# Degrees of a graph aggregation from sums over source tiles made on GpSimd, and one fp32 product with ones for each block

## The chip, the cores and the metric

The kernel runs on one core of a Trainium2 chip. The metric is the device time of one execution in microseconds (us). The core has five engines that work at the same time and are kept in step by semaphores: TensorE (PE), VectorE (DVE), ScalarE (ACT), GpSimd (POOL) and SyncE (SP, which only issues transfers).

## The reference

Two graph layers follow each other on 1250 nodes with 512 features and 20000 edges. The part that the change touches is the first layer's mean over incoming edges: the sum of the messages of a destination is divided by its degree, the number of edges that end in it, but at least 1.

```
msg = xn[edge_index[0]]                                          # xn: batch-normed relu(layernorm(x))
agg = segment_sum(msg, edge_index[1], num_segments=N)
deg = segment_sum(ones((E,)), edge_index[1], num_segments=N)
agg = agg / maximum(deg, 1.0)[:, None]
conv_out = relu(agg @ W_conv + b_conv)
...                                                              # linear attention over the first 256 nodes, h_attn
x = x + batchnorm(conv_out + h_attn + h)                         # first layer
h = maximum(layernorm(x), 0.0)
agg = segment_sum(h[src], dst, num_segments=N)                   # second layer
x = x + relu(batchnorm(relu(batchnorm(((1 + eps) * h + agg) @ W1 + b1)) @ W2 + b2))
```

## The kernel before

**The adjacency.** The 1250 nodes are ten tiles of 125 (`T`, `L`). The kernel builds the matrix `AT`, of 125 partitions by ten source tiles by 1250 destinations: how many edges go from a source to a destination, in fp16. Aggregation then is a product with `AT`. The destinations are cut into 25 windows of 50 (`NW`, `W`), and each window `t` goes through three engines. DVE writes 0/1 rows: `S` for the source's lane (L976) and eight rows of `ring` for tile and destination (L980, called one-hots here). PE multiplies them into counts (eight products, `ring,S`). ACT copies the counts into `AT` (L584), which raises the semaphore `s_at` by one. `ATlo` holds what fp16 can't; its products run only where some count is that large (`If_lt(big_r, most_r)`), which these edges don't ask for.

**The slots.** Between the counts of two windows PE does other work. The table `SLOTS` (L76) names it, slot `t` before the counts of window `t`. The names that matter here: `G7`, `G8`, `G9` are the convolution products of node tiles 7 to 9 (12 products each); `R6` and so on take the rounding remainder of such a tile; `UQ`, `QT`, `MX`, `KV`, `O`, `TA`, `WO` are steps of the attention; `A00` is the aggregate of feature block 0 over destination block 0 (20 products), `D0`, `D1`, `D2` are the degrees of the three destination blocks (`COLS`: 0 to 449, 450 to 849, 850 to 1249), `F1` and `F2` the mean square of the second layer's two weights. D0 stands in slot 18, D1 in slot 23, D2 in the list `LAST` behind the windows.

**What feeds G.** For tile `i`, ACT norms the tile (`hn`, L681), DVE splits it in `hn_hi` and `hn_lo` (L1094, L1095, in the function `normed_parts`), and PE's `G` waits for the second (`s_hns`). DVE's list in window `t` is: `S` and the eight one-hots of window `t + 1`, the split of tile `t - 7`, then the slot's reductions. In window 14 these are the maxima of `UQ2` (`qmax`, `nbq`), which ACT's exponentials (`qf`) wait for; ACT norms tile 8 behind them.

**A degree.** PE multiplies a matrix of ones with `AT` for each of the ten source tiles and sums in PSUM, so that all 128 partitions hold the degree (L1552). ACT copies it to `rdb` (D0, D1), DVE takes the maximum with 1 and the reciprocal (L1034, L1035). Every engine works through its own list in the order in which the program writes it, and waits on semaphores.

**GpSimd** does the scales of norms: for the first layer, then for the two weights (`mean_w`, `scale_w`, L517, L518, behind `F1` and `F2`), then small things of the later stages, with two large ones: the rows `x1 + h` (L529) and the low halves `a_lo` (L557).

Of the kernel before, what the change touches and what calls it, by code (L numbers as in the profile page):

```python
# [5 lines left out]
F32 = mybir.dt.float32  # L6
# [5 lines left out]
ALU = mybir.AluOpType  # L12
# [3 lines left out]
P = 128  # L16
# [3 lines left out]
N, D, HID, E = 1250, 512, 1024, 20000  # L20
# [5 lines left out]
T = 10  # L26
L = N // T
# [6 lines left out]
W = 50  # L34
# [118 lines left out]


SQ1_AT, HIGH1_AT = (20, 21), (23, 24)
RAW = [name for slot in SLOTS for name in slot if name[0] == "A"]
OUT_TILES = [(0, 4), (4, 8), (8, 10)]

# [33 lines left out]
def gnn_kernel(nc, x, src, dst, params, eps, w_conv, wq, wk, wv, wo, proj, w1, w2, out):  # L192
    with ExitStack() as ctx:
        sems = {}

        def sem(name):
            if name not in sems:
                sems[name] = ctx.enter_context(nc.semaphore(name))
            return sems[name]

        def place(name, shape, dt, kib):

            pad = nc.sbuf_tensor(name + "_at", [P, int(kib * KIB)], U8)
            pad.__enter__()
            it = nc.sbuf_tensor(name, shape, dt)
            t = it.__enter__()
            it.__exit__(None, None, None)
            pad.__exit__(None, None, None)
            return t
# [4 lines left out]
        ones16 = place("ones16", [P, P], F16, 3.25)  # L214
        zeros16 = place("zeros16", [P, 1], F16, 3.5)
# [6 lines left out]
        ones32 = place("ones32", [P, 1], F32, 7.9375)  # L222
# [41 lines left out]
        AT = place("AT", [L, T, N], F16, 8)  # L264
        ATlo_all = place("ATlo", [L, T * N], F8, 32.5)
        ATlo = ATlo_all[:].rearrange("p (t n) -> p t n", t=T)
# [44 lines left out]
        st_1 = place("st_1", [P, FB, T, 6], F32, 108)  # L311
        tmpr = place("tmpr", [P, 2, COLS[0][1]], F32, 109.1875)
        aggf = place("aggf", [P, 4, COLS[0][1]], F32, 130.75)
        rdb = place("rdb", [P, N], F32, 146)
        x1 = place("x1", [L, T, D], F32, 154)

        w1_s = [place(f"w1_s{half}", [P, 2, HID], F32, at) for half, at in enumerate((92, 162))]
# [26 lines left out]
        def open_group(eng, name):  # L344
            bank, turn = PLACE[name]
            if turn:
                eng.wait_ge(free[bank], turn)
            return banks[bank]
# [97 lines left out]
        def _(pool):  # L446
            own = Own(pool, sem("own_pool"))
# [63 lines left out]
            factor = wscale[:, 0:1].broadcast_to([P, FB])  # L511
            pool.tensor_tensor(bn_0[:, 0, :], bn_s[:, 0:FB], factor, ALU.mult).then_inc(sem("s_bn0"), 1)
            pool.tensor_tensor(bn_0[:, 1, :], bn_t[:, 0:FB], factor, ALU.mult).then_inc(sem("s_bn0"), 1)
            for layer in range(2):
                pool.wait_ge(sem(f"s_mean_w{layer}"), 1)
                m, s = mean_w[layer], scale_w[layer]
                own.step(pool.tensor_scalar(m[:, 1:2], m[:, 0:1], 1e-30, None, ALU.add))  # L517
                pool.tensor_tensor(s[:, 0:1], m[:, 1:2], minus_half[:, 0:1], ALU.pow).then_inc(sem(f"s_scale_w{layer}"), 1)  # L518
            for f in range(FB - 1):
                pool.wait_ge(sem("s_mv2"), f + 1)  # L520
                batch_scales(f, 1, pcol("n2g", f), pcol("n2b", f), sem("s_bn2"))
# [18 lines left out]
            n = 0  # L540
# [848 lines left out]
        def _(pe):  # L1389
            def mm(o, l, r, start, stop):  # L1390
                return pe.matmul(o, l, r, start=start, stop=stop, skip_group_check=True)  # L1391
# [11 lines left out]
            ps = open_group(pe, "codes")  # L1403
            for a, k in enumerate((1, 2)):
                pe.transpose(ps[0:CH, a * NCH:a * NCH + P], code_r[:, k, 0, :], ident[:])
                ins = pe.transpose(ps[0:CH, a * NCH + P:(a + 1) * NCH], code_r[0:rest, k, 1, :],
                                   ident[0:rest, 0:rest])
            close_group(ins, "codes")
            ps = open_group(pe, "ranges")
            for a in range(2):  # L1410
                mm(ps[0:NH, a * NCH:a * NCH + P], wm[:, a, 0:1].broadcast_to([P, NH]), ident[:], True, True)
                ins = mm(ps[0:NH, a * NCH + P:(a + 1) * NCH], wm[0:rest, a, 1:2].broadcast_to([rest, NH]),
                         ident[0:rest, 0:rest], True, True)
# [42 lines left out]
            def attention(name):  # L1456
# [4 lines left out]
                if name in ("F1", "F2"):  # L1461
                    layer = int(name[1]) - 1
                    pe.wait_ge(sem(f"s_ssq_w{layer}"), 2)
                    ps = open_group(pe, name)[:, 0:1]
                    for half in range(2):
                        ins = mm(ps, ssq_w[layer][:, half:half + 1].broadcast_to([P, P]), ones32[:], half == 0, half == 1)
                    close_group(ins, name)
                    return
                if name[0] == "G":
# [9 lines left out]
                    ps = open_group(pe, name)  # L1479
                    n = 0  # L1480
                    if i == 0:
                        for k in range(FB):
                            ins = mm(ps[0:L, :], hn[:, 0, k, :], wC[:, k, :], k == 0, k == FB - 1)
# [59 lines left out]
                elif name[0] == "D":  # L1543
# [4 lines left out]
                    if name == "D0":  # L1548
                        released("P")
                        pe.load([most_r], most[0:1, 0:1])  # L1550
                    ps = open_group(pe, name)
                    ins = accumulate([(ps[:, 0:w], [(ones16[0:L, :], AT[:, k, c0:c0 + w]) for k in range(T)],  # L1552
                                       [(ones16[0:L, :], ATlo[:, k, c0:c0 + w]) for k in range(T)])])[0]
                elif name[0] == "N":
                    a = int(name[1])
                    for half in range(2):
# [83 lines left out]
            def accumulate(groups):  # L1640

                for ps, pairs, _ in groups:
                    mm(ps, *pairs[0], True, False)
                with pe.If_lt(big_r, most_r):
                    for ps, _, extra in groups:
                        for l, r in extra:
                            mm(ps, l, r, False, False)
                pe.end_ifs()
                last = []
                for ps, pairs, _ in groups:  # L1650
                    for n, (l, r) in enumerate(pairs[1:]):
                        ins = mm(ps, l, r, False, n == len(pairs) - 2)
                    last.append(ins)
                return last
# [187 lines left out]
```

## Time and profile before

| | us |
|---|---|
| median of 3 runs | 367.86 (367.85 to 368.13) |
| the profiled execution | 367.88, of which span 366.0 |
| PE busy | 352.8 (96%) |
| DVE busy | 239.9 (66%) |
| ACT busy | 185.7 (51%) |
| GpSimd busy | 94.6 (26%) |
| mean granted TensorE clock | 0.999 of full speed |

The span goes from the first to the last instruction. Shares are of the span. A product's row lasts longer than the distance to the next one, since products are pipelined: what one costs is read from start to start. A line such as L1391 is that of a helper through which nearly all products go, so rows are told apart by their operands.

### The profile page before, as it was taken

The numbers are of one execution on the slowest core, as the hardware profiler recorded it, in microseconds if no ns is written. First come the engines' busy times: TensorE is split into PE (matmuls) and PEld (weight loads), VectorE is DVE, ScalarE is ACT, GpSimd is POOL, SyncE is SP. The second block draws the span as 40 slices with busy tenths as digits, with TensorE's granted clock in tenths as the row PEclk, the third lists the DMA queues.
The fourth block names the chain that finished last, engine by engine and source line by source line (L and its number), as shares of the span: only waits on it lengthen the run. The fifth ranks groups of instructions, "written<-read, shape, count | busy, mean of one in ns | idle before, by whom it ended". The sixth has DMA issues, their size and how long they took to land.

```text
span 366.0 us, 6163 instructions
## 1 busy us (share of the span) xinstructions
PE 352.8 (96%) x2062; PEld 225.3 (62%) x2062; DVE 239.9 (66%) x650; ACT 185.7 (51%) x311; POOL 94.6 (26%) x163
## 2 busy tenths in 40 slices
PE   7999999989999999999998999999999999999994
PEld 3786655767767666768555665455555555565562
DVE  5889999997877886857987886522465353422324
ACT  1447647779587157465436677411443644333132
POOL 8132120000000000100042678722277565101100
PEclk9999999999999999999999999999999999999999
DMA  6990303300000000024900000000000000010223
GB/s 180 281 298 21 118 2 122 113 3 1 3 4 3 3 3 3 2 71 167 257 19 1 2 0 3 4 2 0 0 3 0 2 0 0 2 49 23 70 56 84
DMA packets 13538, 18.03 MB, mean 49 GB/s; under 512 B 1839, under 2 KB 6895, under 8 KB 13491
## 3 DMA queue, kind: packets, MB, share of 16 engines
q1 hardware_dynamic: 12538, 17.21, 16.4%
q8 instruction: 25, 0.41, 0.5%
q10 hardware_dynamic: 953, 0.23, 0.3%
q14 instruction: 22, 0.18, 0.2%
HBM read 14.88 MB, written 2.56 MB: 48 GB/s over the span
## 4 chain that ended last, share of the span: by engine, by line
PE 72%; DVE 14%; ACT 6%; issue 4%; DVEq 2%; POOL 1%; DMA 0%; SPq 0%; ACTq 0%; POOLq 0%
PE bank L1391 68%; DVE ring L980 2%; DVE st_row L930 1%; ACT hn L681 1%; PE bank L1421 1%; PE bank L1781 1%; PE bank L1743 1%; PE bank L1607 1%; DVE kmax L996 1%; DVEq L1129 1%; DVE st L1087 1%; DVE wC_lo L1241 1%; POOL ln_s L483 1%; DVE hn_lo L1095 1%; DVE hl L1271 1%
## 5 line engine op out<-in xcount | busy, mean ns | idle before, releaser
L1391 PE MATMUL bank<-AT,hh 125*128 125x400 f16 (+1 forms) x240 | 81.0, 340 | 1.5 <-DVE hl L1271 1.2
L1391 PE MATMUL bank<-AT,hl 125*128 125x400 f16 (+1 forms) x240 | 80.8, 339 | 0.0
L980 DVE TENSOR_SCALAR ring<-iota_code,code 125x250 f16<-125x250 f16 x200 | 46.1, 306 | 1.8 <-issue 1.8
L1391 PEld LDWEIGHTS bank<-AT,hh 125*128 125x128 f16 x240 | 23.2, 97 | 20.2 <-DVE hl L1271 1.6
L1391 PEld LDWEIGHTS bank<-AT,hl 125*128 125x128 f16 x240 | 23.4, 97 | 18.0 <-issue 0.2
L1391 PE MATMUL bank<-ring,S 125*128 125x250 f16 x200 | 33.5, 310 | 0.0
L1391 PE MATMUL bank<-a_hi,w_hi 128*128 128x400 f16 (+1 forms) x96 | 32.6, 340 | 0.0
L1391 PE MATMUL bank<-agg_hi,w_hi 128*128 128x400 f16 (+1 forms) x96 | 32.6, 340 | 0.0
L1391 PE MATMUL bank<-a_hi,w_lo 128*128 128x400 f16 (+1 forms) x96 | 32.5, 339 | 0.0
L1391 PE MATMUL bank<-agg_hi,w_lo 128*128 128x400 f16 (+1 forms) x96 | 32.5, 339 | 0.0
L1391 PE MATMUL bank<-agg_lo,w_hi 128*128 128x400 f16 (+1 forms) x96 | 32.5, 339 | 0.0
L1391 PE MATMUL bank<-a_lo,w_hi 128*128 128x400 f16 (+1 forms) x96 | 32.5, 339 | 0.0
L517 POOL TENSOR_SCALAR mean_w<-mean_w 128x1 f32<-128x1 f32 x2 | 0.9, 448 | 121.3 <-ACT mean_w L584 121.3
L1391 PEld LDWEIGHTS bank<-ring,S 125*128 125x128 f16 x200 | 25.8, 145 | 9.0 <-issue 1.7
L853 ACT ACTIVATE zr<-bank,par,undo_w 128x400 f32<-128x400 f32 (+1 forms) x24 | 16.0, 690 | 23.5 <-POOL a_lo L557 17.1
L557 POOL TENSOR_TENSOR a_lo<-zr,a_hi 128x1250 f16<-128x1250 f32 x7 | 22.0, 3142 | 16.7 <-DVE a_hi L1313 16.7
L1082 DVE BATCH_NORM_STATS2 st_f<-zr 128x6 f32<-128x400 f32 (+1 forms) x24 | 13.5, 588 | 18.1 <-ACT zr L853 18.1
L877 ACT ACTIVATE ur<-bank,par,undo_w 128x400 f32<-128x400 f32 (+1 forms) x12 | 8.2, 697 | 32.7 <-PE bank L1391 22.2
L492 POOL TENSOR_TENSOR bn_tmp<-var_eps,minus_half 128x1 f32<-128x1 f32 (+1 forms) x15 | 8.7, 581 | 54.1 <-DVE var_eps L1101 54.1
L976 DVE TENSOR_TENSOR S<-iota_lane,slo 125x1024 f16<-125x1024 f16 x25 | 18.6, 744 | 5.9 <-PE bank L1391 3.5
L483 POOL TENSOR_TENSOR ln_s<-ln_tmp,minus_half 125x1 f32<-125x1 f32 x20 | 14.5, 724 | 24.3 <-DVE ln_tmp L926 24.3
L584 ACT ACTIVATE AT<-bank 125x500 f16<-125x500 f32 x25 | 15.2, 606 | 10.6 <-PE bank L1391 10.4
(230 smaller groups left out, 708.5 us busy)
## 6 DMA issues: line engine op xcount, KB each, us to landing
w_s<-w SPq DMA_DIRECT2D x4, 1024.0 KB, 5.1
x_in<-x SPq DMA_DIRECT2D x5, 448.0 KB
x<-x SPq DMA_DIRECT2D x2, 1120.0 KB
out<-x SPq DMA_DIRECT2D x6, 224.0 KB
wB<-wk SPq DMA_DIRECT2D x1, 1024.0 KB, 8.7
wA<-wq SPq DMA_DIRECT2D x1, 1024.0 KB, 13.9
wC<-w_conv SPq DMA_DIRECT2D x1, 1024.0 KB, 16.3
wB<-wv SPq DMA_DIRECT2D x1, 1024.0 KB, 7.6
```

What stands on the lines that cost most here:

```text
L483: own.step(pool.tensor_tensor(s, ln_tmp[:, 0, i:i + n], minus_half[0:L, 0:n], ALU.pow))
L492: own.step(pool.tensor_tensor(bn_tmp[:, 1, k:k + n], var_eps[:, k:k + n], minus_half[:, 0:n], ALU.pow))
L557: pool.tensor_tensor(a_lo[:, b, :], zr[:, b % 2, :], a_hi[:, b, :], ALU.subtract)\
L584: return act.activation(o, i, ACT.Copy, scale=scale)
L681: ins = act.activation(hn[:, i % 2, f, :], hT[:, f, i * L:(i + 1) * L], ACT.Identity, bias=b[:, f:f + 1], scale=s[:, f:f + 1])
L853: ins = act.activation(zr[:, b % 2, c0:c0 + w], ps[:, 0:w], ACT.Identity, bias=pcol("b1", b), scale=undo_w[0][:, 0:1])
L877: ins = act.activation(ur[:, f % 2, c0:c0 + w], ps[:, 0:w], ACT.Identity, bias=pcol("b2", f), scale=undo_w[1][:, 0:1])
L930: own.step(dve.bn_stats(st_row[:, i % 2, :], x_tile(i)))
L976: dve.tensor_tensor(S[:, slot], iota_lane[0:CH], a, ALU.is_equal)
L980: return dve.tensor_scalar(ring[:, slot, j, a:b], iota_code[0:CH, a:b], code[:, bass.ds(c + j, 1)], float(-CODES * t), ALU.subtract, ALU.i ...
L1082: return dve.bn_stats(st_f[:, f, ci, :], ap)
L1391: return pe.matmul(o, l, r, start=start, stop=stop, skip_group_check=True)
```

## The change

GpSimd now sums `AT` over the ten source tiles, for 100 destinations at a time (13 groups, the last of 50), in fp32. It takes four sums: five tiles plus five tiles (`deg_1`), two plus two of these (`deg_2`), the two results, and the fifth. The result is `degs`, one value for each of 125 lanes and 1250 destinations, in the memory of `rdb`. A group begins when the windows that it reads are copied, and not before 14 are (`DEGREES_FROM`). `s_degs` counts the groups. PE waits for the groups of its block and makes one fp32 product of `degs` with ones in place of ten fp16 products; a product with one column of zeros closes the group in PSUM, since the `ATlo` products between the two are left out or not by a branch. On GpSimd the scale of the first of the second layer's weights now stands behind the eleventh group, that of the other behind the last.

```diff
--- before.py
+++ after.py
@@ -153,6 +153,8 @@
 
 
 SQ1_AT, HIGH1_AT = (20, 21), (23, 24)
+
+DEGREES_FROM = 14
 RAW = [name for slot in SLOTS for name in slot if name[0] == "A"]
 OUT_TILES = [(0, 4), (4, 8), (8, 10)]
 
@@ -311,7 +313,11 @@
         st_1 = place("st_1", [P, FB, T, 6], F32, 108)
         tmpr = place("tmpr", [P, 2, COLS[0][1]], F32, 109.1875)
         aggf = place("aggf", [P, 4, COLS[0][1]], F32, 130.75)
+
         rdb = place("rdb", [P, N], F32, 146)
+        degs = place("degs", [L, N], F32, 146)
+        deg_1 = place("deg_1", [L, T // 2, 2 * W], F32, 150.90625)
+        deg_2 = place("deg_2", [L, 2, 2 * W], F32, 152.875)
         x1 = place("x1", [L, T, D], F32, 154)
 
         w1_s = [place(f"w1_s{half}", [P, 2, HID], F32, at) for half, at in enumerate((92, 162))]
@@ -511,11 +517,30 @@
             factor = wscale[:, 0:1].broadcast_to([P, FB])
             pool.tensor_tensor(bn_0[:, 0, :], bn_s[:, 0:FB], factor, ALU.mult).then_inc(sem("s_bn0"), 1)
             pool.tensor_tensor(bn_0[:, 1, :], bn_t[:, 0:FB], factor, ALU.mult).then_inc(sem("s_bn0"), 1)
-            for layer in range(2):
+            def weight_scale(layer):
                 pool.wait_ge(sem(f"s_mean_w{layer}"), 1)
                 m, s = mean_w[layer], scale_w[layer]
                 own.step(pool.tensor_scalar(m[:, 1:2], m[:, 0:1], 1e-30, None, ALU.add))
                 pool.tensor_tensor(s[:, 0:1], m[:, 1:2], minus_half[:, 0:1], ALU.pow).then_inc(sem(f"s_scale_w{layer}"), 1)
+
+            def source_sums(n, c0, w):
+
+                half = T // 2
+                if n:
+                    pool.wait_ge(sem("s_degs"), n)
+                pool.wait_ge(sem("s_at"), max(DEGREES_FROM, -(-(c0 + w) // W)))
+                own.step(pool.tensor_tensor(deg_1[:, :, 0:w], AT[:, 0:half, c0:c0 + w], AT[:, half:T, c0:c0 + w], ALU.add))
+                own.step(pool.tensor_tensor(deg_2[:, :, 0:w], deg_1[:, 0:2, 0:w], deg_1[:, 2:4, 0:w], ALU.add))
+                own.step(pool.tensor_tensor(deg_2[:, 0, 0:w], deg_2[:, 0, 0:w], deg_2[:, 1, 0:w], ALU.add))
+                pool.tensor_tensor(degs[:, c0:c0 + w], deg_2[:, 0, 0:w], deg_1[:, 4, 0:w], ALU.add)\
+                    .then_inc(sem("s_degs"), 1)
+
+            groups = [(c0, min(2 * W, N - c0)) for c0 in range(0, N, 2 * W)]
+            for n, (c0, w) in enumerate(groups):
+                source_sums(n, c0, w)
+                if c0 + w == 1100:
+                    weight_scale(0)
+            weight_scale(1)
             for f in range(FB - 1):
                 pool.wait_ge(sem("s_mv2"), f + 1)
                 batch_scales(f, 1, pcol("n2g", f), pcol("n2b", f), sem("s_bn2"))
@@ -1548,9 +1573,14 @@
                     if name == "D0":
                         released("P")
                         pe.load([most_r], most[0:1, 0:1])
-                    ps = open_group(pe, name)
-                    ins = accumulate([(ps[:, 0:w], [(ones16[0:L, :], AT[:, k, c0:c0 + w]) for k in range(T)],
-                                       [(ones16[0:L, :], ATlo[:, k, c0:c0 + w]) for k in range(T)])])[0]
+                    pe.wait_ge(sem("s_degs"), -(-(c0 + w) // (2 * W)))
+                    ps = open_group(pe, name)[:, 0:w]
+                    mm(ps, ones32[0:L, 0:1].broadcast_to([L, P]), degs[:, c0:c0 + w], True, False)
+                    with pe.If_lt(big_r, most_r):
+                        for k in range(T):
+                            mm(ps, ones16[0:L, :], ATlo[:, k, c0:c0 + w], False, False)
+                    pe.end_ifs()
+                    ins = mm(ps[:, 0:1], ones16[0:L, :], zeros16[0:L, 0:1], False, True)
                 elif name[0] == "N":
                     a = int(name[1])
                     for half in range(2):
```

PE's list where D0 stands (`degs` against `ones`), before:

```order
L1391 MATMUL bank<-hh,neg_id 125x512 [waits s_gh]
L1550 TENSOR_LOAD most [waits s_lo1,free6,s_lo0,s_at]
L1391 MATMUL bank<-AT,ones 128x450 [waits free7]
L1644 COMPARE_AND_BRANCH
L1391 MATMUL bank<-ATlo,ones 128x450 x10
L1644 UNCONDITIONAL_BRANCH
L1391 MATMUL bank<-AT,ones 128x450 x9
L1678 TENSOR_LOAD win [waits s_lo1,s_at]
```

and now:

```order
L1416 MATMUL bank<-hh,neg_id 125x512 [waits s_gh]
L1575 TENSOR_LOAD most [waits s_lo1,free6,s_lo0,s_at]
L1416 MATMUL bank<-degs,ones 128x450 [waits free7,s_degs]
L1579 COMPARE_AND_BRANCH
L1416 MATMUL bank<-ATlo,ones 128x450 x10
L1579 UNCONDITIONAL_BRANCH
L1416 MATMUL bank<-zeros,ones 128x1
L1708 TENSOR_LOAD win [waits s_lo1,s_at]
```

Nine products in a row are gone behind the branch, a closing one of one column stands there, and the first waits for GpSimd too.

GpSimd's list between the first layer's scales (`bn`) and those of the weights, before:

```order
L512 TENSOR_TENSOR bn<-bn_s,wscale 128x4 [waits s_bn1]
L513 TENSOR_TENSOR bn<-bn_t,wscale 128x4
L517 TENSOR_SCALAR mean_w<-mean_w 128x1 [waits s_mean_w0]
L518 TENSOR_TENSOR scale_w<-mean_w,minus_half 128x1 [waits own_pool]
L517 TENSOR_SCALAR mean_w<-mean_w 128x1 [waits s_mean_w1]
```

and now (the first two groups of sums, and the end of the eleventh):

```order
L519 TENSOR_TENSOR bn<-bn_t,wscale 128x4
L532 TENSOR_TENSOR deg<-AT 125x500 [waits s_at]
L533 TENSOR_TENSOR deg<-deg 125x200 [waits own_pool]
L534 TENSOR_TENSOR deg<-deg 125x100 [waits own_pool]
L535 TENSOR_TENSOR degs<-deg 125x100 [waits own_pool]
L532 TENSOR_TENSOR deg<-AT 125x500 [waits s_at,s_degs]
...
L535 TENSOR_TENSOR degs<-deg 125x100 [waits own_pool]
L523 TENSOR_SCALAR mean_w<-mean_w 128x1 [waits s_mean_w0]
L524 TENSOR_TENSOR scale_w<-mean_w,minus_half 128x1 [waits own_pool]
L532 TENSOR_TENSOR deg<-AT 125x500 [waits s_at,s_degs]
```

Eleven groups of four sums stand ahead of the first weight's scale, two more ahead of the second's. The lists of DVE and ACT stay as they were.

## Rows read from the trace of the kernel before

**Rows 1.** Page: chain by engine; then busy time (instructions) of two stretches.
```profile
PE 72%; DVE 14%; ACT 6%; issue 4%; DVEq 2%; POOL 1%; DMA 0%; SPq 0%; ACTq 0%; POOLq 0%
...
core 0: us, PE busy (x) PEld busy (x) DVE busy (x) ACT busy (x) POOL busy (x), PEclk, DMA share, GB/s
95.70:119.20 23.50, 22.70 (x140) 16.69 (x139) 18.33 (x62) 16.86 (x38) 0.00 (x0) 1.00 0.01 3
119.20:191.30 72.10, 72.10 (x444) 48.31 (x443) 57.30 (x124) 34.47 (x48) 5.88 (x14) 1.00 0.23 67
```

**Rows 2.** Timeline of PE at D0, D1, D2: start us, us, operation, idle before.
```profile
119.29 2.06 PE L1391 MATMUL bank<-AT,ones 125*128 125x450 f16 x10
121.19 1.33 PE L1391 MATMUL bank<-ring,S 125*128 125x250 f16 x8
...
148.59 1.86 PE L1391 MATMUL bank<-AT,ones 125*128 125x400 f16 x10
150.28 0.33 PE L1391 MATMUL bank<-AT,hh 125*128 125x400 f16 x1
...
176.05 1.85 PE L1391 MATMUL bank<-AT,ones 125*128 125x400 f16 x10
```

**Rows 3.** Timeline of PE: the fp32 products of WO0, WO1.
```profile
165.39 7.07 PE L1391 MATMUL bank<-attnT,wA 128*128 128x256 f32 x32
...
172.29 0.34 PE L1391 MATMUL bank<-AT,hh 125*128 125x400 f16 x1
```

**Rows 4.** Timeline of GpSimd: a sum with one element, one with 1250.
```profile
261.61 0.19 POOL L494 TENSOR_TENSOR bn_tmp<-mv_f,bn_s 128x1 f32<-128x1 f32 x1
261.88 0.19 POOL L495 TENSOR_TENSOR bn_t<-par,bn_tmp 128x1 f32<-128x1 f32 x1
...
281.07 2.56 POOL L557 TENSOR_TENSOR a_lo<-zr,a_hi 128x1250 f16<-128x1250 f32 x1 [2.39 <-DVE a_hi L1313]
```

**Rows 5.** Timelines of DVE and GpSimd where they work at the same time.
```profile
223.72 0.69 DVE L1271 TENSOR_TENSOR hl<-hring,hh 125x512 f16<-125x512 f32 x1
226.74 1.33 DVE L1271 TENSOR_TENSOR hl<-hring,hh 125x512 f16<-125x512 f32 x1 [2.33 <-ACT hh L826]
...
225.04 2.49 POOL L529 TENSOR_TENSOR x<-x,hring 125x512 f32<-125x512 f32 x2
...
52.45 0.36 POOL L495 TENSOR_TENSOR bn_t<-par,bn_tmp 128x4 f32<-128x4 f32 x1
```

**Rows 6.** Timeline of DVE, windows 14 to 17.
```profile
98.48 0.68 DVE L1095 TENSOR_TENSOR hn_lo<-hn,hn_hi 128x500 f16<-128x500 f32 x1
...
101.39 0.16 DVE L1012 SCALAR_TENSOR_TENSOR nbq<-diag,qmax 128x2 f32<-128x2 f32 x1
102.17 0.69 DVE L976 TENSOR_TENSOR S<-iota_lane,slo 125x1024 f16<-125x1024 f16 x1 [0.62 <-PE bank L1391]
...
106.26 0.42 DVE L1094 CAST hn_hi<-hn 128x500 f16<-128x500 f32 x1 [1.53 <-ACT hn L681]
106.72 0.68 DVE L1095 TENSOR_TENSOR hn_lo<-hn,hn_hi 128x500 f16<-128x500 f32 x1
...
110.12 0.68 DVE L1095 TENSOR_TENSOR hn_lo<-hn,hn_hi 128x500 f16<-128x500 f32 x1
...
112.62 1.85 DVE L980 TENSOR_SCALAR ring<-iota_code,code 125x250 f16<-125x250 f16 x8 [0.20 <-issue]
```

**Rows 7.** Timelines of PE (first products of G7, G8, G9) and ACT.
```profile
102.07 0.38 PE L1391 MATMUL bank<-wC_hi,hn_hi 128*125 128x512 f16 x1
...
107.51 0.39 PE L1391 MATMUL bank<-wC_hi,hn_hi 128*125 128x512 f16 x1
...
112.37 0.38 PE L1391 MATMUL bank<-wC_hi,hn_hi 128*125 128x512 f16 x1
...
95.13 0.60 ACT L584 ACTIVATE AT<-bank 125x500 f16<-125x500 f32 x1 [0.57 <-PE bank L1391]
...
102.55 0.47 ACT L646 ACTIVATE qf<-bank,nbq 128x256 f32<-128x256 f32 x1
```

**Rows 8.** Timeline of DVE at the first layer's end.
```profile
191.55 0.58 DVE L1179 TENSOR_TENSOR tmpr<-bank,rdb 128x400 f32<-128x400 f32 x1 [0.96 <-PE bank L1391]
```

## The prediction, made before the changed kernel ran

> **What bounds the kernel now.** I read the chain of waits first: 72% of the span runs through PE, most of it through its products [rows 1]. Then the table of busy time by stretch. From 119.20 to 191.30 us PE is busy 72.10 of 72.10 us, so time taken off its list there comes off the run, and any wait put before it is added to the run. From 95.70 to 119.20 us PE is busy 22.70 of 23.50 us and DVE 18.33, while GpSimd does nothing at all. Both lie at the full granted clock (1.00). The reader should see two things in these rows: PE is the bound through the whole change, and DVE, in the stretch where GpSimd is to start working, has only 5.2 us in which it is idle.
>
> **What leaves PE.** The three degree groups D0, D1 and D2 are ten fp16 products each [rows 2]: 119.29 to 121.19 is 1.90 us, 148.59 to 150.28 is 1.69, and D2 at 176.05 has the row of D1's shape, so 1.69 too. Together 5.28 us. The branch inside them costs nothing visible: 1.90 us for 4500 columns is 0.42 ns a column, as in the products around it.
>
> **What PE gets.** One fp32 product for each group. Its price is read from the last attention products: 32 records of 256 columns, two to a product, from 165.39 to 172.29, so 6.90 / 16 = 0.431 us for 256 columns or 1.68 ns a column [rows 3]. 1250 columns cost 2.10 us. The closing product has one column and a weight load of its own. From above it is bounded by one of the eight products of 250 columns (1.33 / 8 = 0.17 us [rows 2]), from below by nothing. I take 0.10, as what loading the weights leaves of it: 0.3 us for three. Total 2.4, **saving 2.9 us** (between 2.7 and 3.2). The branch now stands behind the fp32 product; it costs nothing as long as that product (0.76 us, four times the one that covered it) hides it, and at most a few tenths if not.
>
> **What GpSimd gets.** Four sums for each of 13 groups. One element takes 0.19 us, 1250 take 2.56 [rows 4], so 1.90 ns an element over 0.19: 1.14 us for 5x100 elements, 0.57 for 2x100, 0.38 and 0.38 for the two of 100. With 0.08 between (the small rows stand 0.27 apart, at 261.61 and 261.88, less 0.19) a group is 2.8 us. The inputs of the first sum are fp16, which no GpSimd row has; its price lies between 0.6 (half) and 1.3. GpSimd is busy 0.00 and 5.88 us of the two stretches [rows 1], so the time is there. Groups 0 to 6 all become due at once, when the copy of window 13 (from 95.13 us) is in [rows 7], and the rest follow two windows apart.
>
> **Do the new waits of PE end late?** D0 wants group 4. Alone, five groups take 14 us from 95.7 and end at 110, 9 us before D0. D1 wants group 8, due before D0 and used 29 us later. D2 wants group 12, due with the last copy of counts, before the output products of the attention, which alone take 6.9 us. The scale of the second layer's first weight now stands behind group 10 on GpSimd; that group is due a window before the mean for which the scale waits. I put all four at zero; if a group were late, the counts of the next window, and with them everything on PE, would queue behind D0.
>
> **What it does to DVE.** This is the term that decides. GpSimd's adds and DVE meet once in this trace [rows 5]. DVE's difference of two SBUF tensors takes 0.69 us alone and took 1.33 when it began at 226.74 inside an add of GpSimd that ended at 225.04 + 2.49 = 227.53. It lost 0.64 and so came free about 0.14 before the add's end. So DVE stood still while GpSimd read. Does that hold for DVE's one-hots (`ring`), the bulk of its work? A product of four elements on GpSimd took 0.36 instead of some 0.2 when only one-hots ran beside it [rows 5], so a one-hot does hold GpSimd up; that GpSimd holds a one-hot up is not in the trace, since nothing long ran on GpSimd then. I take it that it goes both ways.
>
> The Trainium skill, "SBUF — State Buffer", section "Who interferes with whom", speaks against this change: DVE and GpSimd share one pair of ports under an exclusive lock, DVE instructions with two SBUF inputs and one-source ones in a two-port mode (tensor_scalar among them) contend, and the one that came second waits for the whole instruction. The trace agrees for two inputs (0.64 us lost); no row shows the one-hot as the second. By the rule my forecast stands; if it ended at two-input instructions, the second case below would.
>
> Now the walk. A group of sums blocks DVE for 1.00 + 0.43 + 0.24 + 0.24 = 1.9 us (each sum less 0.14), and in each gap of 0.22 us DVE gets one or two one-hots through (0.23 each: 1.85 / 8) [rows 6].
> - Window 14. When GpSimd begins, eight one-hots and the two halves of the split of tile 7 (hn_hi, hn_lo) stand before DVE. About six sums slip between them: 3.3 us, of which 0.4 falls on idle time. The split ends at 102.0 instead of 98.48 + 0.68 = 99.16 [rows 6]. PE wants it at 102.07 (G7) [rows 7]: covered. But the maxima of UQ2 end at 104.4 instead of 101.55; ScalarE takes them from 102.55, and its norm of tile 8 moves by about 2.
> - Window 15. DVE begins at 104.5 instead of 102.17 and loses another 2.3 us in the one-hots, less the 1.53 us for which it waited before tile 8 [rows 6]. The split of tile 8 is 3.1 us late. G8 followed it by 0.11 us (107.40 to 107.51) [rows 6, 7]: **PE loses 3.1**.
> - Window 16. Ten more contending instructions, 3.4 us more: the split of tile 9 is 6.6 late. It ended at 110.80, 1.57 us before G9 at 112.37. **PE has lost 5.0.**
> - Later. The seven due groups run out near 121 us. The one-hots of window 18 ended at 114.47 and PE counts them at 121.19, 6.7 us later, which covers DVE's further delay, and the six late groups meet a DVE that waits for PE. At the end of the stretch DVE waited 0.96 us for the last A product [rows 8]; DVE's list there moves with D0 and D1, so D2's saving of 1.0 uses that up and costs nothing above 0.1.
>
> Sum: 5.0 - 2.9 = **2.1 us slower**. The profiled run took 367.88 us (span 366.0) and the median of the runs is 367.86, so the forecast is 367.88 + 2.1 = 370.0, and the same for the median. The term of 5.0 is soft: with sums of 0.9/0.45/0.3/0.3 us the same walk gives 2.5, with 1.25 us for the first sum 5.8. The case's own range is 367.9 to 372.
>
> **Rivals.**
> - Faster: GpSimd doesn't hold one-hots up, only the two-input instructions. Then in each window at most two of them wait, mostly under idle time, and PE loses some 0.3: 367.88 - 2.9 + 0.3 = 365.3. For it: no row shows a one-hot held. Against it: the four elements that a one-hot did hold up.
> - Faster or equal, held but mildly: the fp16 sums are cheap, near 0.6 to 0.9 us, or more one-hots slip into a gap. PE loses 1 to 2.5: 366.0 to 367.5.
> - Slower still: if the gap between two sums is a little shorter than a one-hot, exactly one gets in. The split of tile 7 is then 5.2 us late and PE stalls there already, 2.3; by G9 it has lost 10, net 375. It decides from a gap under 0.2 us, and I have 0.22. Stalls of 3 us may also lower TensorE's clock, which costs further time; the stretch of the walk holds 0.8 us of idle PE in all, at full clock [rows 1], so no row prices that.
> - The change doing nothing: excluded, since PE's list is shorter by 24 products.
>
> **Chances.** The forecast 0.42, faster without the hold 0.33, mild hold 0.15, strict alternation 0.10. Two in ten may lie outside: the range is 364.8 to 373.5. A measurement can tell about 0.2% (0.74 us) from no change. Faster than 367.1: all of the second case and half of the mild one, 0.40. Within 0.2%: the other part of the mild one and the foot of the forecast, 0.12. Slower: 0.48.
>
> **What would show it.** In the new profile: D0 to D2 at 0.8 to 0.9 us each (right or wrong for the 2.9). The first sum at 1.1 us on GpSimd. In 96 to 118 us the `ring` rows of DVE at two or three times 1.85 us for eight, and PE idle before G8 and G9, put down to DVE's hn_lo. If the `ring` rows stay at 1.85, the walk is wrong and the time is near 365.3. If GpSimd's sums take two or three times their price while DVE keeps its pace, DVE wins the port each time: also 365.3, unless group 4 then misses D0.

## The result, and the profile after

The changed kernel takes **372.61 us** (median of 4 runs, 372.60 to 373.80) where the kernel before takes 368.0 (4 runs, 367.85 to 368.35): a ratio of 1.0125, 95% interval 1.0093 to 1.0156. It is slower, as forecast, and 2.6 us above the 370.0 that the prediction named, inside its range of 364.8 to 373.5, though not inside the 367.9 to 372 that it gave its main case. The profiled execution took 372.6 us with a span of 370.8, against 367.88 and 366.0: 4.8 us more.

The busy time of the stretches of [rows 1] in the changed kernel, with two stretches more (columns as there):

```profile
core 0: us, PE busy (x) PEld busy (x) DVE busy (x) ACT busy (x) POOL busy (x), PEclk, DMA share, GB/s
95.70:119.20 23.50, 20.34 (x106) 13.67 (x106) 22.92 (x51) 13.96 (x33) 21.22 (x29) 0.93 0.01 2
119.20:191.30 72.10, 72.10 (x448) 49.38 (x447) 64.31 (x133) 36.08 (x54) 23.20 (x33) 1.00 0.23 67
112.00:114.00 2.00, 2.00 (x6) 1.12 (x5) 2.00 (x6) 0.00 (x0) 1.88 (x2) 0.50 0.00 0
235.00:240.00 5.00, 5.00 (x22) 2.36 (x21) 1.30 (x3) 1.65 (x3) 3.51 (x4) 0.78 0.00 0
```

In the first stretch DVE is now busy 22.92 of 23.50 us, for fewer instructions (51 for 62), GpSimd 21.22, and PE gets through 106 products where it did 140. The last two rows are new: TensorE's granted clock falls to half, once at 112 us and once near 235.

DVE's timeline, which answers to [rows 6]:

```profile
96.24 2.98 DVE L1005 TENSOR_SCALAR ring<-iota_code,code 125x250 f16<-125x250 f16 x8 [0.19 <-issue]
99.13 1.24 DVE L1119 CAST hn_hi<-hn 128x500 f16<-128x500 f32 x1
100.41 0.98 DVE L1120 TENSOR_TENSOR hn_lo<-hn,hn_hi 128x500 f16<-128x500 f32 x1
...
104.86 3.26 DVE L1005 TENSOR_SCALAR ring<-iota_code,code 125x250 f16<-125x250 f16 x8
108.04 0.61 DVE L1119 CAST hn_hi<-hn 128x500 f16<-128x500 f32 x1
108.69 1.39 DVE L1120 TENSOR_TENSOR hn_lo<-hn,hn_hi 128x500 f16<-128x500 f32 x1
```

Eight one-hots take 2.98 to 3.26 us where they took 1.85, and the splits 1.24 + 0.98 and 0.61 + 1.39 where they took 0.42 + 0.68. Durations (ns) of all 200 one-hots, least, median and most; then three single one-hots out of the row of 104.86, and the two sums that they met:

```profile
L1005 DVE TENSOR_SCALAR ring<-iota_code,code x200: 274/290/1064, 15.4 to 154.5; 125x250 f16<-125x250 f16 x100
...
105.46 1.06 DVE L1005 TENSOR_SCALAR ring<-iota_code,code 125x250 f16<-125x250 f16 x1
106.45 0.34 DVE L1005 TENSOR_SCALAR ring<-iota_code,code 125x500 f16<-125x500 f16 x1
106.71 0.63 DVE L1005 TENSOR_SCALAR ring<-iota_code,code 125x250 f16<-125x250 f16 x1
...
105.28 1.16 POOL L532 TENSOR_TENSOR deg<-AT 125x500 f32<-125x500 f16 x1
106.52 0.73 POOL L533 TENSOR_TENSOR deg<-deg 125x200 f32<-125x200 f32 x1
```

The one-hot that begins 0.18 us into a sum ends 0.08 us behind it (106.52 against 106.44, then 107.34 against 107.25). The next one begins where the sum ends and takes 0.34 us, as it does without GpSimd. So two one-hots pass for each sum, one held and one not.

GpSimd's sums pay too. The first three sums, and the last sum of the twelfth group, with the instruction of DVE that it met:

```profile
95.79 1.15 POOL L532 TENSOR_TENSOR deg<-AT 125x500 f32<-125x500 f16 x1 [42.35 <-ACT AT L609]
97.01 0.73 POOL L533 TENSOR_TENSOR deg<-deg 125x200 f32<-125x200 f32 x1
97.82 0.52 POOL L534 TENSOR_TENSOR deg<-deg 125x100 f32<-125x100 f32 x1
...
160.80 2.32 POOL L535 TENSOR_TENSOR degs<-deg 125x100 f32<-125x100 f32 x1
...
160.50 2.37 DVE L1082 SCALAR_TENSOR_TENSOR w_lo<-w_s,scale_w,w_hi 128x2048 f16<-128x2048 f32 x1
```

The wait of a sum lies in its own duration. A sum of 100 elements takes 0.40 us where it isn't held (at 160.32, ahead of that of 160.80; DVE's instruction began behind it), 0.52 between one-hots, and 2.32 when it comes second to one instruction of DVE with two inputs.

PE at G8, D0, and at the late place (as in [rows 2, 7]):

```profile
108.03 0.43 PE L1416 MATMUL bank<-hh,neg_id 125*125 125x512 f16 x1 [1.45 <-ACT hh L609]
110.17 0.40 PE L1416 MATMUL bank<-wC_hi,hn_hi 128*125 128x512 f16 x1 [1.71 <-issue]
...
112.09 0.63 PE L1416 MATMUL bank<-wC_hi,hn_hi 128*125 128x512 f16 x1
112.52 0.63 PE L1416 MATMUL bank<-wC_lo,hn_hi 128*125 128x512 f16 x1
...
123.66 0.92 PE L1416 MATMUL bank<-degs,ones 125*128 125x450 f32 x2
124.41 0.17 PE L1416 MATMUL bank<-zeros,ones 125*128 125x1 f16 x1
124.44 1.37 PE L1416 MATMUL bank<-ring,S 125*128 125x250 f16 x8
...
230.51 0.33 PE L1416 MATMUL bank<-AT,hl 125*128 125x400 f16 x1
233.02 0.34 PE L1416 MATMUL bank<-AT,hh 125*128 125x400 f16 x1 [2.17 <-issue]
```

From these rows and those of before the 4.8 us can be followed:

| place on PE | before | after | behind by |
|---|---|---|---|
| first product of G8 | 107.51 | 110.17 | 2.66 |
| counts behind G8 | 110.11 | 114.47 | 4.36 |
| D0 | 119.29 | 123.66 | 4.37 |
| counts behind D0 | 121.19 | 124.44 | 3.25 |
| D2 | 176.05 | 178.39 | 2.34 |
| first turned tile behind the first layer | 195.49 | 196.94 | 1.45 |
| end of the span | 366.0 | 370.8 | 4.8 |

Four pieces: the wait before G8 (2.7), G8's products at 0.43 us from start to start in place of 0.215 from its fourth on (1.7), the shorter degrees (-2.9), and 3.4 us in the second layer, where nothing of the change is near. The label "issue" on the wait of 110.17 means that the trace names no releaser; the split of tile 8 ended at 108.69 + 1.39 = 110.08, 0.09 ahead of it.

### The profile page after: what moved, and what is told of

Its sections match the earlier page's. It is cut to its first block, busy times and chain, and to the rows that moved or that the text cites. A ratio compares the mean times of both kernels' runs of the same rounds, so it can differ in the third digit from the quotient of the medians.

```text
span 370.8 us, 6187 instructions
## 1 busy us (share of the span) xinstructions
PE 354.2 (96%) x2041; PEld 224.9 (61%) x2041; DVE 253.0 (68%) x650; ACT 185.9 (50%) x311; POOL 134.8 (36%) x215
## 4 chain that ended last, share of the span: by engine, by line
PE 65%; DVE 20%; ACT 6%; issue 5%; DVEq 2%; POOL 1%; DMA 0%; SPq 0%; ACTq 0%; POOLq 0%
PE bank L1416 61%; DVE ring L1005 2%; DVE st_f L1107 2%; DVE st_row L955 1%; PE bank L1446 1%; ACT hn L706 1%; PE bank L1811 1%; PE bank L1773 1%; DVE hT L1206 1%; DVE hn_lo L1120 1%; DVE tmpr L1204 1%; DVE rdb L1060 1%; PE bank L1637 1%; DVE qmax L1036 1%; DVE kmax L1021 1%
## 5 line engine op out<-in xcount | busy, mean ns | idle before, releaser
L1416 PE MATMUL bank<-AT,hh 125*128 125x400 f16 (+1 forms) x240 | 82.1, 344 | 3.3 <-issue 2.2
L1005 DVE TENSOR_SCALAR ring<-iota_code,code 125x250 f16<-125x250 f16 x200 | 53.5, 341 | 1.6 <-issue 1.6
L532 POOL TENSOR_TENSOR deg<-AT 125x500 f32<-125x500 f16 (+1 forms) x13 | 14.4, 1109 | 65.4 <-ACT AT L609 64.8
L1001 DVE TENSOR_TENSOR S<-iota_lane,slo 125x1024 f16<-125x1024 f16 x25 | 20.3, 811 | 3.6 <-issue 1.9
L1324 DVE SCALAR_TENSOR_TENSOR aggf<-bank,agg_terms,hT 128x400 f32<-128x400 f32 (+1 forms) x12 | 7.8, 651 | 19.5 <-PE bank L1416 18.5
## 6 DMA issues: line engine op xcount, KB each, us to landing
out<-x SPq DMA_DIRECT2D x6, 224.0 KB
```

Source lines behind the costliest of these rows:

```text
L532: own.step(pool.tensor_tensor(deg_1[:, :, 0:w], AT[:, 0:half, c0:c0 + w], AT[:, half:T, c0:c0 + w], ALU.add))
L1001: dve.tensor_tensor(S[:, slot], iota_lane[0:CH], a, ALU.is_equal)
L1005: return dve.tensor_scalar(ring[:, slot, j, a:b], iota_code[0:CH, a:b], code[:, bass.ds(c + j, 1)], float(-CODES * t), ALU.subtract, ALU.i ...
L1324: ins = dve.scalar_tensor_tensor(aggf[:, k % 4, 0:w], ps[:, 0:w], agg_terms[:, 1:2], hT[:, f, c0:c0 + w], ALU.mult, ALU.add).then_inc(sem( ...
```

## The experiments

In each diff the lines are of the changed kernel unless said otherwise. Beside each group the kernel before ran on the same chip, at 367.97 to 368.12 us.

**The sums and the product, each alone.** `e1_no_sums` leaves out the four sums of each group, so its degrees are all one.

```diff
-                own.step(pool.tensor_tensor(deg_1[:, :, 0:w], AT[:, 0:half, c0:c0 + w], AT[:, half:T, c0:c0 + w], ALU.add))
...
-                pool.tensor_tensor(degs[:, c0:c0 + w], deg_2[:, 0, 0:w], deg_1[:, 4, 0:w], ALU.add)\
-                    .then_inc(sem("s_degs"), 1)
+                pool.memset(degs[:, c0:c0 + w], 1.0).then_inc(sem("s_degs"), 1)
```

> The changed kernel, with GpSimd's four sums of each group left out: it fills the 13 pieces of degs with ones instead (so the degrees, and what is computed with them, are others). PE's program is that of the changed kernel to the instruction. Theory (the sums hold DVE up, and PE starves before G7 to G9, at a falling clock): no wait before G8, ring rows of 1.85 us for eight, full clock until 190 us, and PE some 2.9 us ahead of the kernel before at 191 us. The stall of 2.17 us at 230.8 us, which waits for nothing that the profile shows, I take for PE's own instructions coming in late: then it stays, with the clock halved behind it, and the time is 367.9 - 2.9 + 3.4 = 368.4. Rival (the late stall follows from the earlier delay of GpSimd and DVE): it goes too, 365.0. Rival (the fp32 product and its branch cost PE more than I read): PE is less than 2.5 us ahead at 191 us.

Measured 368.48 us (ratio 1.0, interval 0.9974 to 1.0027). PE starts D0 at 119.29 as before, is done with it at 120.08, and one-hots are back at 1.85 us for eight. At the first turned tile it is at 192.57, 2.92 us ahead of the kernel before: that is what the shorter degrees save. Yet the time is no better, since the late idle time is there without any sums, with the clock's fall behind it:

```profile
228.94 0.34 PE L1412 MATMUL bank<-AT,hh 125*128 125x400 f16 x1 [2.46 <-issue]
```

Busy time of the stretch behind it:

```profile
230.00:235.00 5.00, 5.00 (x19) 2.25 (x18) 2.07 (x4) 2.19 (x4) 3.67 (x4) 0.66 0.02 3
```

`e2_sums_only` is the kernel before with the sums beside it, whose result nothing reads.

> The kernel before, with GpSimd's sums of the changed kernel added at the same places; nobody uses their result (the last of the four goes into deg_1), and D0 to D2 are the ten fp16 products. Theory: the whole loss of the first part is here. G8 starts 2.7 us late and runs at half clock, D0 is 4.4 us late, as in the changed kernel, and nothing is saved: 367.9 + 4.4 = 372.3. PE's program is that of the kernel before, so no late stall. Rival (the loss needs PE's new wait for degs or the fp32 products): within 0.7 of 367.9.

Measured 372.16 us (1.0103, 1.0075 to 1.0131). The rows before G8 are those of the changed kernel, and the late idle time isn't there:

```profile
108.06 0.43 PE L1413 MATMUL bank<-hh,neg_id 125*125 125x512 f16 x1 [1.45 <-ACT hh L606]
110.20 0.66 PE L1413 MATMUL bank<-wC_hi,hn_hi 128*125 128x512 f16 x1 [1.71 <-issue]
...
235.24 0.54 PE L1413 MATMUL bank<-AT,hh 125*128 125x450 f16 x2 [0.31 <-DVEq L1324]
```

So the sums alone cost 4.0 us (4.04 by the traces at the first turned tile). The shorter list gains 2.9 and pays 3.4 at the late place. 368.0 + 4.0 - 2.9 + 3.4 gives 372.5, the changed kernel's time.

**The late stall.** `e3_pad` lengthens PE's list at its start.

```diff
             keep_busy(SPARE["start"], banks[0])
+            for _ in range(21):
+                mm(banks[0][:, 0:1], ones16[:], ones16[:, 0:1], True, True)
```

> The changed kernel with 21 products of one column at the start of PE's program, where PE waits anyway for the first transposes. They bring the rest of the program back to about the place in memory that it had in the kernel before (the change takes 60 instructions, weight loads counted, and adds 18). Theory (the late stall is a matter of where PE's instructions lie): the stall of 2.17 us at 230.8 us and the half clock behind it are gone, 372.6 - 3.4 = 369.2. Rival (it is a wait for data): it stays, 372.6 or a little more.

Measured 369.27 us (1.003, 0.9997 to 1.0064), 3.3 less than the changed kernel, for work added. The trace shows 0.32 us idle in place of 2.17, at full clock. `e6_no_sums_pad` puts the same 21 products into `e1_no_sums`.

> As e1_no_sums (the sums of GpSimd left out, degrees set to one), with 21 one-column products at PE's start as in e3_pad. Theory: without the sums the only cost left in e1_no_sums was the stall near 229 us with the fall of the clock behind it, and that hangs on where PE's list stands. So 21 products more at the start take it away, and the saving of 2.9 us on PE comes out whole: 367.88 - 2.9 = 365.0, no idle time over 0.4 us in 225 to 240 us. Rival (the stall comes from being 2.9 us earlier at that place, with a transfer of the next stage not in yet): it stays, 368.5.

Measured 364.94 us (0.9915, 0.9897 to 0.9933): the saving of 2.9 us comes out whole, and being early at that place isn't the cause. It gets there as early as `e1_no_sums` (225.68 and 225.58 us). `e9_before_104` and `e10_before_52` put 104 and 52 such products into the kernel *before*, which has nothing of the change.

> The kernel before, its degrees as they were, with 104 one-column products on PE at the start. Theory (the late stall hangs on where PE's list stands against the blocks of 16 KB in which it is fetched): in the kernel before PE does 128 products with as many weight loads between two such fetches (246.50 to 268.60 us), so about 128 products more or less change nothing and 104 more are as good as 24 fewer. 24 fewer is what the changed kernel has, and it stalled. So this kernel, which has nothing of the change, stalls behind the branch of the second layer's row block 9: 2.0 to 2.5 us idle and labelled issue, with the clock at half for some 3 us behind it. One such product costs 0.094 us at the start (21 took 7.35 - 5.37 us there), 9.8 us, of which 1.2 fall on idle time: 367.97 + 8.6 + 3.4 = 380.0. Rival (the stall is of the change itself, or of the time at which PE gets there): no such idle time, 376.5.

> The kernel before with 52 one-column products on PE at the start, the control for e9_before_104. By the theory of fetched blocks this is as good as 76 fewer or 52 more, neither near the 24 fewer at which the changed kernel stalled: the place behind the branch of row block 9 stays at 0.3 us and at full clock; 4.9 us at the start, 1.2 of them hidden: 367.97 + 3.7 = 371.7. Rival (any shift of some size brings the stall): 2 us idle there, 375.1. A stall at another place, behind another branch, would speak for the theory too, and its place would say how far into a block the bad position lies.

One run each: 370.47 and 367.81 us beside 368.03. PE's timelines, first of the one with 104, then with 52:

```profile
231.12 0.35 PE L1391 MATMUL bank<-AT,hl 125*128 125x450 f16 x1
233.21 0.34 PE L1391 MATMUL bank<-AT,hh 125*128 125x400 f16 x1 [1.74 <-issue]
```

```profile
231.22 0.54 PE L1391 MATMUL bank<-AT,hh 125*128 125x450 f16 x2 [0.41 <-DVEq L1302]
```

The stall is in the kernel before too once its list is moved by 104 products, in the same row block, four products further on, and not when it is moved by 52. The expectation counts 24 products fewer in the changed kernel; by the page it is 21 (2062 and 2041 records, an fp32 product being two), so 107 more (128 less 21) would be the same place, and with three less PE should stop some three products later, which is about what is seen. Both times were forecast wrong (380.0 and 371.7), since the cost of the added products was: 104 delay PE's next work by 2.2 us (9.72 for 7.56), not by 8.6, and 52 by 0.4. Whether PE stalls is read from the rows, and doesn't hang on that. One thing differs: here 1.74 us of idle time left the clock at 1.00, where 2.17 and 2.46 were followed by its fall.

What lies there: PE comes to a branch (`agg1_extra`, ahead of the last row block of the second layer) that skips 120 products, starts the row block of twelve behind it and stops within it. Queue 8 of the profile, kind instruction, moved two packets of 16 KB in the kernel before in the 6.6 us up to there, and none in the changed kernel in 17.6 us; its next came in at 230.7, when PE had stopped. From the view of DMA queues, before (224.0 to 230.6 us) and after (213 to 230.6, then 213 to 231):

```profile
q8 instruction: 2, 0.03, 1.7%
```

```profile
q14 instruction: 2, 0.02, 0.3%
...
q8 instruction: 1, 0.02, 0.3%
```

Between two such packets of the kernel before (246.5 and 268.6 us) PE does 128 products with their weight loads:

```profile
246.50:268.60 22.10, 22.10 (x128) 12.22 (x127) 8.49 (x14) 7.06 (x10) 7.93 (x8) 1.00 0.00 0
```

That the stall hangs on where PE's list stands is shown by the kernels with and without it. That PE waits for its own instructions to come in is inferred from this coincidence; no row names the releaser.

**The clock.** `e5_warm` fills the idle time ahead of G8 with spare products.

```diff
-                        pe.wait_ge(sem("s_hns"), i)
+                        if i != 8:
+                            pe.wait_ge(sem("s_hns"), i)
...
+                    if i == 8:
+                        keep_busy(7, banks[7])
+                        pe.wait_ge(sem("s_hns"), i)
+                        ps = banks[7]
...
+                    if i == 7:
+                        keep_busy(8, open_group(pe, "G8"))
                     pe.wait_ge(sem("s_gh"), i + 1)
```

> As the changed kernel, with 15 spare products on PE in the idle time before G8: 8 of 450 columns (0.19 us each, 1.5 us) while it waits for R7, 7 (1.3 us) while it waits for the split of tile 8. They go into G8's bank, which G8 then overwrites. Theory (the idle time of PE before G8 made the granted clock fall to half): the waits stay, G8 begins near 110.2 us as in the changed kernel, but its 12 products take 2.60 us instead of 4.30 and the clock stays at 1.00: 1.7 us less. Rival (DVE's and GpSimd's work next to it sets the clock, or the clock falls here whatever PE does): 110 to 114 stays at 0.5 to 0.9, nothing gained. The stall of 2.2 us and the clock's second fall near 231 us hang on where PE's list stands, by my theory, and there are 15 products more in it ahead of that place: if they are gone, another 3.4 us. So 370.9 with the late stall, 367.5 without it; by the rival 372.6 or 369.2.

Measured 369.09 us (1.0031, 1.0015 to 1.0046). The clock stays at 1.00. PE's timeline:

```profile
110.69 0.38 PE L1416 MATMUL bank<-wC_hi,hn_hi 128*125 128x512 f16 x1
...
113.28 1.34 PE L1416 MATMUL bank<-ring,S 125*128 125x250 f16 x8
...
115.33 0.38 PE L1416 MATMUL bank<-hh,neg_id 125*125 125x512 f16 x1
115.73 0.40 PE L1416 MATMUL bank<-wC_hi,hn_hi 128*125 128x512 f16 x1
```

Busy time of a stretch of G8:

```profile
112.00:114.00 2.00, 2.00 (x12) 1.39 (x11) 2.00 (x5) 0.52 (x1) 1.87 (x2) 1.00 0.00 0
```

So PE's idle time brought the fall, and not the work of the others beside it. But of the 1.7 us only 0.5 came back (196.43 for 196.94 at the first turned tile): the spare products overshot the split by 0.5 us, and G9, which stands 0.22 us behind the product ahead of it in the kernel before, stands 0.40 behind it here. Its split ended at 115.63. With G8 at full speed the split of tile 9 is the next thing late; in the changed kernel the slow G8 had hidden that. The late stall is gone with 15 products more in the list, as in `e3_pad`, which makes up the other 3 us. The 367.5 that I expected was 1.6 too low.

**Where the sums stand.** `e4_d0_before` leaves D0 as it was and sums only for D1 and D2, from window 17 on.

```diff
-DEGREES_FROM = 14
+DEGREES_FROM = 17
...
-            groups = [(c0, min(2 * W, N - c0)) for c0 in range(0, N, 2 * W)]
+            groups = [(c0, min(2 * W, N - c0)) for c0 in range(COLS[1][0], N, 2 * W)]
```

> The changed kernel, but D0 is made by ten fp16 products as before, and GpSimd sums only the 800 destinations of D1 and D2, in eight groups that begin when 17 windows are copied (112 us instead of 95.8), where DVE has waited for PE by turns. Theory: DVE is held up as much per group, but its lead covers that, so PE is never short of a split tile: no stall before G8 and G9, PE 1.8 us ahead of the kernel before at 191 us, 366.1 where no late stall is, 369.5 with it. Rival (the holds reach PE wherever the sums stand, by the lanes and one-hots of the windows): PE idle between 112 and 165 us, 368 or more without a late stall.

Measured **366.06 us** (0.9959, 0.9923 to 0.9996): faster than both kernels, though the interval ends just under 1 (four of the ten runs took 367.6 to 369.3). GpSimd works on the sums from 112.41 us, the one-hots beside it take as long as in the changed kernel, and PE waits nowhere longer than in the kernel before. A row of DVE's timeline, and one of the busy times:

```profile
112.87 2.98 DVE L1005 TENSOR_SCALAR ring<-iota_code,code 125x250 f16<-125x250 f16 x8 [0.20 <-issue]
```

```profile
119.20:191.30 72.10, 72.10 (x440) 48.12 (x439) 64.63 (x131) 34.76 (x48) 25.22 (x39) 1.00 0.24 67
```

`e7_from12` keeps all thirteen groups and all three products, starts D0's five groups earlier and the others not before window 17; `e8_from10` starts the five earlier still. Both have the 21 products of `e3_pad` at their start, so that the late stall stays away.

```diff
-DEGREES_FROM = 14
+DEGREES_FROM = 12, 17
...
-                pool.wait_ge(sem("s_at"), max(DEGREES_FROM, -(-(c0 + w) // W)))
+                pool.wait_ge(sem("s_at"), max(DEGREES_FROM[n > 4], -(-(c0 + w) // W)))
```

> All 13 groups of sums, but the five that D0 needs begin when 12 windows are copied (84.0 us) instead of 14, and the others not before 17; with the 21 one-column products at the start. Theory (a sum costs PE only where DVE has no slack before the next split): from 84 to 96 us DVE is idle for 3.1 of 12 us in the kernel before, and its splits stand 1.9 to 4.6 us ahead of G; five groups run until about 100, so the split of tile 7 is late by up to 2.9 us and still covered, and G8 waits for 0 to 1 us more than before. Clock full throughout. 365.0 to 366.0, best guess 365.3. Rival (any overlap of the sums with DVE costs its full length): five groups cost 2.7 us wherever they lie, 367.7 or more.

> As e7_from12, but the five groups of D0 begin when 10 windows are copied (72.7 us). There DVE is busy 9.29 of 10 us (70 to 80 us) and PE already waits 0.97 us for DVE's hn_lo at 78.71. Theory (slack decides): DVE loses about 1.3 us in each eight one-hots and 0.5 in a split until 88.7, and the splits for G3 and G4 come 2 to 3 us later, all of it on PE: G products near 78.7 us begin at about 81, 365.3 + 2.3 = 367.6; a fall of the clock behind that wait would add 1.7, 369.3. Rival (the sums only cost where they fall together with the maxima and exponentials of window 14 and tile 8): 365.3, as e7_from12.

Measured 366.25 us (0.9952, 0.9934 to 0.997) and 368.65 (1.0021, 1.0008 to 1.0035). PE, first of `e7_from12`, then of `e8_from10`:

```profile
108.60 0.43 PE L1416 MATMUL bank<-hh,neg_id 125*125 125x512 f16 x1 [1.45 <-ACT hh L609]
108.87 0.39 PE L1416 MATMUL bank<-wC_hi,hn_hi 128*125 128x512 f16 x1
```

```profile
80.73 0.40 PE L1416 MATMUL bank<-wC_hi,hn_hi 128*125 128x512 f16 x1 [2.98 <-DVE hn_lo L1120]
```

and the busy times of `e8_from10` behind that wait:

```profile
82.00:84.00 2.00, 2.00 (x6) 1.07 (x5) 2.00 (x6) 0.00 (x0) 1.84 (x3) 0.50 0.03 8
```

From 84 us on most of the hold falls on DVE's idle time: G8 is 1.36 us late (108.87 for 107.51) and not 2.66, and the clock stays up. The time is 0.95 above the best guess and just outside the 365.0 to 366.0 expected, so slack alone doesn't make the five groups free. From 72.7 us on, where DVE had hardly any idle time, PE waits 2.98 us in place of 0.97 at G3 and its clock falls for some 3 us; the forecast of 367.6 to 369.3 holds, and the rival that only the place near tile 8 is sensitive falls. At D0 PE is behind by 3.7 us with D0's groups from window 10 (123.00), by 1.4 from window 12 (120.66), and by 4.4 in the changed kernel, where two more groups follow at once.

## Why the prediction was right, and where it was off

- **PE is the bound through the change.** Right: the delay behind G8 is still there at D0 (4.36, 4.37), and from 119.20 to 191.30 PE is busy all the time [rows 1].
- **What leaves PE, 2.9 us.** Right: D0 takes 0.78 us (123.66 to 124.44) for 1.90, D1 0.76 (151.87 to 152.63) and D2 0.78 (178.39 to 179.17) for 1.69 each, 2.96 in all, and `e1_no_sums` is 2.92 ahead. The price taken from WO's fp32 products [rows 3] fits 450 columns (0.75 us for 0.76) and is somewhat low for 400 (0.73 and 0.75 for 0.67). The closing product costs 0.03 and not 0.10. The branch cost nothing where it stands.
- **Four sums of 1.14, 0.57, 0.38 and 0.38 us.** Nearly: unheld they take 1.03, 0.61, 0.40 and 0.40. The fp16 inputs make little difference. Beside a busy DVE a group takes 3.1 to 3.9 us from start to start, forecast 2.8.
- **The new waits of PE end in time.** Right. The second layer's first scale, at 151.01 us, wasn't late either.
- **GpSimd holds one-hots up, and they hold it up.** Right, and this decided the sign. The rule cited from the Trainium skill ("SBUF — State Buffer", section "Who interferes with whom") agrees with the trace here: a one-input one-hot is among the held ones (the longest took 1064 ns).
- **The size of the hold: the term that was mis-sized.** The walk gave 2.3 us for each eight one-hots with GpSimd in between; they lose 1.1 to 1.4. The walk let the four sums of a group block DVE for 1.9 us, with one or two one-hots in each gap. The rows show two for each sum, so eight meet just one group, and the held one of each pair (0.28 us unheld) loses 0.78 us to the sum of 5x100 (1.06), 0.35 to that of 2x100 (0.63) and 0.14 to each of 100 (0.42, at 107.51): 1.4 us. The sum pays as well, 0.12 us of its own. The split of tile 7 came at 101.39, covered as forecast (102.0), the maxima of UQ2 ended at 104.04 (104.4 forecast), and G8 was 2.66 us late, 3.1 forecast.
- **G9 another 1.9 us late, 5.0 in all.** The total is near by luck: G9 is behind by 4.37 (116.74), as much as the counts ahead of it, but it waited for nothing of its own. Two errors met. DVE lost less than forecast, and PE's half clock made G8 longer by 1.7 us, in which DVE caught up. `e5_warm` shows what is left of the step at full clock: D0 3.55 us late, of which 0.5 are the spare products' own. So the step of 5.0 should have been some 3.0, and the clock made it 4.4.
- **The clock.** It stood among the rivals without a price, with the remark that stalls of 3 us may lower it. Two waits of 1.45 and 1.71 us with one product between them did, and `e5_warm` shows that they were the cause.
- **A term that the sum doesn't have.** It has nothing for PE behind the first layer, and this is the largest miss: 3.4 us at 231, from 21 products fewer in PE's list (my 24 took an fp32 product for one record). No view read of the kernel before would have given it. Without it the time is 369.27 us (`e3_pad`), 0.7 under the forecast; with it the time is above the 372 of the main case, and lies in the wider range by luck, as no case that the range was drawn for had such a stall.
- **The end of the first layer.** Right: D2's saving brings PE 0.9 us forward there (2.34 to 1.45), and the 0.96 us for which DVE waited for PE [rows 8] are used up.

The rivals: without a hold the time would have been 365.3, and the one-hots exclude that. `e6_no_sums_pad`, with no hold since it has no sums, took 364.94. Strict alternation, one one-hot for each sum, is excluded by the two that pass. The mild hold (1 to 2.5 us on PE) named the right cause, more one-hots in a gap, but even at full clock PE was some 3.0 us late at D0 (`e5_warm`), between that case and the forecast.

## What to carry to other kernels

Before work is moved to an idle engine, look for what it shares with the busy one, and price it on both: 3 us of sums on GpSimd cost DVE 1.1 to 1.4 us for each eight one-hots here. Then place it where the held engine has slack before its next due result: D0's five groups cost PE 1.4 us from window 12 and 3.7 from window 10 (with the clock's fall), and those of D1 and D2 nothing from window 17 on. And when a kernel with fewer instructions gets slower far from the edit, look there for idle time that no semaphore explains, and move the list by a few instructions before judging the edit.

## What was not expected of the hardware

- PE stood for 2.17 to 2.46 us (1.74 in `e9_before_104`) behind a branch that skips 120 products, in three kernels and not in nine, by how many products stood in its list: 21 fewer than in the kernel before, or 104 more, brought it; 14 or 6 fewer, as many, or 52 more did not. Between two packets of queue 8 lie 128 products with their weight loads; 21 fewer is the same place in such a stretch as 107 more.
- GpSimd's sums and DVE's one-hots hold each other up, two one-hots to a sum, and both pay: eight one-hots went from 1.85 to 3.26 us, a sum of 100 elements from 0.40 to 0.52, and to 2.32 behind one instruction of DVE of 2.37.
- The granted clock went to half (0.50) for some 3.4 us behind 3.2 us of idle time in two pieces (1.45 and 1.71), behind 1.45 and 0.83 (`e3_pad`, 109.50 us), behind 2.17 and 2.46 us in one, and behind 2.98; it stayed at 1.00 behind 1.74 (`e9_before_104`), and behind 1.45 (`e7_from12`). TensorE's levels are 2.4 and 1.2 GHz; the products went from 0.215 to 0.43 us.
